# Moving the Q projection of the second half into the feature loop of the first, and rotating straight from PSUM

## What is computed

```python
h = _layernorm(x) * (1 + ca) + sa
q = h @ Wq.T + bq;  k = h @ Wk.T + bk;  v = h @ Wv.T + bv      # per head of 128
q = q*cos + _rotate_half(q)*sin;  k = k*cos + _rotate_half(k)*sin
qp, kp = features(q), features(k)     # x/|x|, @ R.T, then [sin, cos]/sqrt(F)
kv = einsum('bhsf,bhsd->bsfd', kp, v);  out = einsum('bhsf,bsfd->bhsd', qp, kv)
x = x + ga * (out @ Wo.T + bo)        # then layer norm 2 and the experts
```

## Time and profile before

| | us |
|---|---|
| median of the runs shown (2 runs: 3911.14 and 4193.43) | 4052.29 |
| the profiled execution, device time | 3917.5 |
| its span, slowest core (core 3) | 3915.9 |
| spans of the 8 cores | 3854.5 to 3915.9 |

### The profile page before, as it was taken

The page is one execution under the profiler, slowest core; times in us unless marked ns, Lnnn a source line. Parts: engine busy times, 40 slices in busy tenths (PEclk is TensorE's granted clock), DMA queues, the critical chain, the costliest instruction groups (busy, mean ns, idle before and its releaser), DMA issues.

```text
span 3915.9 us, 32272 instructions; the slowest of 8 cores (3854.5 to 3915.9 us)
## 1 busy us (share of the span) xinstructions
PE 2514.2 (64%) x10824; PEld 1084.3 (28%) x10824; DVE 1355.2 (35%) x2504; ACT 379.7 (10%) x422; POOL 169.7 (4%) x294
## 2 busy tenths in 40 slices
PE   3349721212982323493299678985899679976886
PEld 1124311101431111141144233432344234432332
DVE  0456255555623444536522122221222022211203
ACT  0111212121111101102100000000000000000000
POOL 0000000000000110000000000000000000000000
PEclk8559855555996566695599889998899789988998
DMA  9513100003325434710053675348543864457547
GB/s 161 104 54 65 25 26 15 27 15 56 56 52 92 85 74 81 174 22 0 16 108 70 131 240 128 75 84 239 172 92 65 184 217 99 92 111 226 156 74 270
DMA packets 84940, 395.10 MB, mean 101 GB/s; under 512 B 7184, under 2 KB 7440, under 8 KB 75312
## 3 DMA queue, kind: packets, MB, share of 16 engines
q0 software_dynamic: 41536, 208.26, 30.7%
q1 hardware_dynamic: 33696, 146.98, 10.9%
q10 hardware_dynamic: 9552, 37.80, 2.8%
HBM read 538.26 MB, written 46.20 MB: 149 GB/s over the span
## 4 chain that ended last, share of the span: by engine, by line
PE 51%; DMA 24%; DVE 13%; issue 8%; ACT 3%; DVEq 0%; POOL 0%; ACTq 0%; POOLq 0%; SPq 0%
PE pb L1034 23%; PE pb L612 9%; PE pb L1110 8%; DMA AW<-wmod 7%; DMA AW<-w2i 5%; DMA AW<-w2scr 5%; PE pb L902 3%; DVE AMS L780 2%; DMA w2scr<-AW 2%; PE pb L429 2%; DMA AW<-w1i 2%; PE pb L578 1%; DMA AW<-w3i 1%; PE pb L548 1%; DVE AMS L1122 1%
## 5 line engine op out<-in xcount | busy, mean ns | idle before, releaser
L1034 PE MATMUL pb<-AHT,AW 128*128 128x512 bf16 x4608 | 1007.8, 381 | 62.0 <-DMA AW<-w1i 39.6
L1110 PE MATMUL pb<-AW,AOT 128*128 128x512 bf16 x2304 | 593.5, 424 | 289.8 <-DMA AW<-w2i 154.3
L1034 PEld LDWEIGHTS pb<-AHT,AW 128*128 128x128 bf16 x4608 | 450.5, 98 | 619.1 <-issue 88.4
L1110 PEld LDWEIGHTS pb<-AW,AOT 128*128 128x128 bf16 x2304 | 241.9, 107 | 641.4 <-issue 432.6
L612 PE MATMUL pb<-AW,AHT 128*128 128x512 bf16 x1536 | 351.4, 382 | 0.0
L1122 DVE TENSOR_TENSOR AMS<-pb,AMS 128x2048 f32<-128x2048 f32 x40 | 91.6, 2291 | 727.8 <-PE pb L1110 724.4
L578 PE MATMUL pb<-identf,AX 128*128 128x128 f32 x256 | 98.6, 445 | 295.9 <-ACT AX L539 244.0
L429 PE MATMUL pb<-AW,scol 128*1 128x512 bf16 x384 | 135.0, 529 | 139.0 <-DMA AW<-wmod 122.9
L1058 ACT ACTIVATE AMS<-AMS 128x1024 f32<-128x1024 f32 x64 | 67.7, 1057 | 1470.2 <-DVE AMS L1055 1470.2
L1060 DVE TENSOR_TENSOR AMS<-pb,AMS 128x1024 f32<-128x1024 f32 x64 | 78.4, 1224 | 373.7 <-PE pb L1034 373.7
L612 PEld LDWEIGHTS pb<-AW,AHT 128*128 128x128 bf16 x1536 | 143.3, 98 | 182.5 <-issue 25.6
(11 more groups left out here) (148 smaller groups left out, 1666.8 us busy)
## 6 DMA issues: line engine op xcount, KB each, us to landing
AW<-w2scr SPq DMA_DIRECT2D x54, 2048.0 KB, 9.4
AW<-wmod POOLq DMA_DIRECT2D x24, 2048.0 KB, 19.4
w2scr<-AW ACTq DMA_DIRECT2D x18, 2048.0 KB
AW<-w1i POOLq DMA_DIRECT2D x32, 1024.0 KB, 8.1
AW<-w3i POOLq DMA_DIRECT2D x32, 1024.0 KB, 8.7
AW<-w2i POOLq DMA_DIRECT2D x16, 2048.0 KB, 24.2
AX<-xin SPq DMA_DIRECT2D x16, 1024.0 KB, 5.0
AW<-wqt POOLq DMA_DIRECT2D x4, 2048.0 KB, 18.2
```

The costliest lines, as they stand in the source:

```text
L1034: ins = tt.matmul(pu[:, th * 512:(th + 1) * 512], slot(sl)[:, ic * 128:(ic + 1) * 128], ahtb[:, ic * 1024 + th * 512: ic * 1024 + (th + 1) ...
L1110: ins = tt.matmul(pw[:, ob * 512:(ob + 1) * 512], hebuf[:, hc * 1024 + tau * 128: hc * 1024 + tau * 128 + 128], slot(ws)[:, ob * 512:(ob + ...
```

## The change

- `emit_qkv_block` is split into `emit_qkv_wdma` (the two loads) and `emit_qkv_chunk` (one tile's matmuls and what follows them). The bias load now takes lanes 4 to 7 as well.
- For q and k, the ACT copy to `srb` is gone in both halves; four of the six rotation operations on DVE read the float32 result in PSUM instead.
- Half 1's two q blocks move into half 0's feature loop: their weight and bias loads are emitted before the loop, and chunks (ob 0, tile t-1) and (ob 1, tile t-1) after `emit_ln1_tile(1, t)` in iterations 1 to 7; the last two come after `emit_mid_B(0, 7)`. Both chunks of an iteration use the same PSUM bank, `pqkv{(t-1)%2}`.
- The k and v blocks of half 1 stay behind the loop. The loads for ob 2 and 3 are emitted after the last q chunks, that for ob 4 after ob 2's chunks, that for ob 5 after ob 3's.

```diff
-        def emit_qkv_block(sh, ob):
+        def emit_qkv_wdma(sh, ob):
             wname, wbi = wsrc[ob]
             wkey = f"awblk{ob % 2}"
             sch.dma("gpsimd", lambda g, wname=wname, wbi=wbi, ob=ob: g.dma_start(
                 blkbuf(ob % 2)[:].rearrange("p (c n) -> p c n", c=NIC),
                 dram[wname][wbi]), lanes=(4, 5, 6, 7),
                 writes=W(ar_aw, wkey, (ob % 2) * 16384, (ob % 2 + 1) * 16384))
...
             sch.dma("gpsimd", lambda g, bsrc=bsrc, ob=ob, brow=brow: g.dma_start(
                 brow, dram[bsrc][0:1, (ob % 2) * 512:(ob % 2) * 512 + 512]),
-                writes=[brkey])
-            for t in range(8):
+                lanes=(4, 5, 6, 7), writes=[brkey])
+
+        def emit_qkv_chunk(sh, ob, t):
...
+            if True:
                 tg = sh * 8 + t
                 pcol = (t % 2) * 512
                 pv = pb0[:, pcol:pcol + 512]
...
-                    srb_ = srb if t % 2 == 0 else amsb[0:128, 14592:15104]
-                    srbk = "srb" + ("A" if t % 2 == 0 else "B")
-                    srb_lo = 19968 if t % 2 == 0 else 29184
-                    sch.op("scalar", lambda s, pv=pv, srb_=srb_: s.copy(srb_[:], pv),
-                           reads=[pk], writes=W(ar_ms, srbk, srb_lo, srb_lo + 1024))
+                    srbk = pk
...
-                    srb3 = srb_[:].rearrange("p (h d) -> p h d", h=4)
+                    srb3 = pv.rearrange("p (h d) -> p h d", h=4)
...
+        emit_qkv_wdma(1, 0)
+        emit_qkv_wdma(1, 1)
         for t in range(8):
             if t:
                 emit_mid_B(0, t - 1)
...
             emit_ln1_tile(1, t, True, None, lnxsA,
                           lambda: W(ar_x1, "lnxs", 57344, 65536),
                           cacol, sacol, ["col1", "col0"], vr=True)
+            if t:
+                emit_qkv_chunk(1, 0, t - 1)
+                emit_qkv_chunk(1, 1, t - 1)
         emit_mid_B(0, 7)
-        for ob in range(6):
-            emit_qkv_block(1, ob)
+        emit_qkv_chunk(1, 0, 7)
+        emit_qkv_chunk(1, 1, 7)
+        emit_qkv_wdma(1, 2)
+        emit_qkv_wdma(1, 3)
+        for t in range(8):
+            emit_qkv_chunk(1, 2, t)
+        emit_qkv_wdma(1, 4)
+        for t in range(8):
+            emit_qkv_chunk(1, 3, t)
+        emit_qkv_wdma(1, 5)
+        for t in range(8):
+            emit_qkv_chunk(1, 4, t)
+        for t in range(8):
+            emit_qkv_chunk(1, 5, t)
```

More of the change, by code:

```diff
@@ L595, in emit_qkv_block @@
                 writes=W(ar_aw, wkey, (ob % 2) * 16384, (ob % 2 + 1) * 16384))
-            isq, isv = ob < 2, ob >= 4
             bsrc = ["bq", "bq", "bk", "bk", "bv", "bv"][ob]
@@ L601, in emit_qkv_block @@
                 brow, dram[bsrc][0:1, (ob % 2) * 512:(ob % 2) * 512 + 512]),
-                writes=[brkey])
-            for t in range(8):
+                lanes=(4, 5, 6, 7), writes=[brkey])
+        def emit_qkv_chunk(sh, ob, t):
+            wkey = f"awblk{ob % 2}"
+            brow = brows[0:1, (ob % 2) * 512:(ob % 2) * 512 + 512]
+            brkey = f"brow{ob % 2}"
+            isq, isv = ob < 2, ob >= 4
+            if True:
                 tg = sh * 8 + t
@@ L657, in emit_qkv_block @@
                         writes=[dkey])
+        def emit_qkv_block(sh, ob):
+            emit_qkv_wdma(sh, ob)
+            for t in range(8):
+                emit_qkv_chunk(sh, ob, t)
         def emit_mid_A(sh, t):
```

## The result

The median of the kernel after is 3953.46 us (12 runs), that of the kernel before 3916.45 us (11 runs). The ratio is 1.0093, with a 95% interval of 1.0068 to 1.0118: about 36 us slower.

The account below looks back on a forecast made before the run. Latency was taken to bound the feature loop, no engine being full, and matmuls the projections; 3917.5 us plus 101.5 (loop), minus 38.4 (tail), minus 4 (bias lane) gave 3977 us, 1.5% more; 8-in-10 range 3945 to 4010.

Parts of the forecast that it names:

- the lower end, 3945: Whole kernel: low end of the 8-in-10 range, 3945 us, for chunks partly hidden in PE's idle time; hiding rival 5%.
- The place, and that nothing hides: Feature loop, behind emit_ln1_tile(1, t): chunks, rotation and products run serially, so PE's 10.0 us gap isn't free for q chunks.
- Price of a pair: Half 0's feature loop: 14.08 us for an iteration's two q chunks, 7 pairs; with bank waits +101.5 us.
- The second chunk at the full clock: Second q chunk of a loop iteration: 3.88 us, the clock still up after 2.5 us of idling; other end 5.58.
- the clock stays down: Rival, loop: half clock in both chunks, +5.06 us a pair, 4014 us (+2.5%); second chunk only, 3989; chance 17%.
- DVE reading PSUM: Rotation's four multiplies: float32 from PSUM costs the same as bf16 from SBUF, no change; upper end 7 us in all.
- The tail: Behind the loop, up to ob 2: fewer chunks left, but PE waits some 11 us for weights; -38.4 us, up to -28.
- The bias row's lane: Loads beside tile 1's x load: bias and second wqt load issued about 6 us earlier; 4 us off, ends 0 and 8.
- the sum itself: Whole kernel: +101.5 - 38.4 - 4 = +59.1 us on 3917.5, giving 3977 us, 1.5% more; forecast's chance 63%.
- a change of about 2%: Whole kernel: what a measurement can tell from none (to 3996 or 3839 us); chance of staying within it 0.80.
- lower ends (3945, 3965): Whole kernel: 3945 us starts the 8-in-10 range, for partial hiding; 3965 starts the forecast's own range, to 3996.

Follow-up runs that it names:

- e7: Kernel after, TensorE's semaphore waited for first, an iteration's two q chunks in two banks of the other PSUM tensor; ratio to kernel before 1.0034, loop 580 us.
- e9: Kernel after with two banks for the q chunks and their rotations emitted behind the products of the next emit_mid_B; ratio to kernel before 0.9896, loop 531 us.
- e6: Kernel after, TensorE's semaphore first, v blocks instead of q blocks in the loop, separate PSUM banks; no ratio, profiled run 3855.14 us, loop 495.4 us.
- e4: Kernel after with its wait order written out, TensorE's semaphore first and VectorE's last; ratio to kernel before 1.0095, loop 600.4 us.
- e2: Kernel before with the wait order written out, TensorE's semaphore first and VectorE's last; ratio to kernel before 0.9927, loop 496.0 us.
- e10: Kernel after with each engine's own semaphore waited for first and, of the others, VectorE's and TensorE's last; ratio to kernel before 1.0048.
- e5: Kernel before with each engine's own semaphore waited for first and, of the others, VectorE's and TensorE's last; ratio to kernel before 0.9884.
- e1: Kernel before with the wait order written out, VectorE's semaphore first and TensorE's last; ratio to kernel before 1.002.
- e3: Kernel after with the wait order written out, VectorE's semaphore first and TensorE's last; ratio to kernel before 1.0241.

## Why the prediction was right or wrong

It said 3977 us, 59 more than before. The time lies 36 us above, inside the range; the sign and the mechanism hold, the size doesn't, by 23 us. That it fell inside the range is luck: the lower end, 3945, stood for chunks that hide in part, and none did.

- **The place, and that nothing hides: right.** The timeline of after shows the chunks, the rotation and the products in a row. e7, e9 and e6 name the cause as the prediction did: the chunks cost 12.0 us a pair without the shared bank, 5.0 with the rotation behind the products, and 0 with nothing on DVE.
- **Price of a pair: right in sum.** +101.5 forecast, +104.4 measured at one wait order (e4 less e2), some 107 at another (e10 less e5). On core 3 the seven first chunks took 5.0 to 6.2 us (5.58 taken, ends 5.09 and 6.07), the gap for the bank 2.40 (2.5), the rotation as computed.
- **The second chunk at the full clock: wrong in part.** On core 3 two of seven second chunks took 5.3 us instead of 3.9, and so on 5 of the 7 other cores. In e4 it was two of seven on seven cores, in e10 three of seven on all eight, always behind the same gap of 2.40 us. The prediction took from the earlier trace rows that the clock holds for 2.7 us of idling, more than the 2.5 of the gap. Busy time by us of core 4 after the first chunk of another iteration, columns as in the earlier trace rows:

```profile
720.00:721.00 1.00, 1.00 (x6) 0.29 (x3) 0.00 (x0) 0.00 (x0) 0.00 (x0) 1.00 0.00 0
721.00:722.00 1.00, 0.23 (x1) 0.00 (x0) 0.67 (x2) 0.00 (x0) 0.00 (x0) 1.00 0.00 0
722.00:723.00 1.00, 0.00 (x0) 0.00 (x0) 0.79 (x3) 0.00 (x0) 0.00 (x0) 1.00 0.00 0
723.00:724.00 1.00, 0.38 (x1) 0.14 (x2) 0.90 (x3) 0.00 (x0) 0.00 (x0) 0.51 0.00 0
```

  PE stopped at 721.23, and at 723.0 the granted clock was down to half (1.2 GHz), after 1.8 us. One observation of 2.7 us was no bound. The miss costs 2 x 1.4 = 2.8 us, about what the loop measured more than the sum, and the third cold chunk of e10 fits its 107. It is a part of the rival "the clock stays down", at 2 of 7.
- **DVE reading PSUM: right, at no cost.** Groups by line, core 4, 520 to 1050 us:

```profile
L641 DVE TENSOR_TENSOR AMS<-pb,cosbuf 128x256 f32<-128x256 f32 x14 | 5.9, 425 | 66.7 <-PE pb L620 66.7
L644 DVE TENSOR_TENSOR AMS<-pb,sinbuf 128x256 f32<-128x256 f32 x14 | 5.8, 415 | 0.0
```

  425 and 415 ns out of PSUM, and 425 and 417 in the kernel before out of SBUF. By the estimate from the table in the Trainium skill, "VectorE: DVE Perf Modes", section "The TRN2 errata — SBUF-src ops pay a fixed extra latency per instruction", each would have been 0.065 us longer; neither size of operation shows it here.
- **The tail: right.** Ob 2 was to start 23.7 us after the loop, behind some 11 us of idling. It started 19.4 to 23.9 us after it, behind 7.2 to 11.7 us of idling (by core), and the slowest core is at the upper end. PE on core 4:

```profile
1057.17 5.27 PE L617 MATMUL pb<-AW,AHT 128*128 128x512 bf16 x15 [0.22 <-issue]
...
1065.15 3.61 PE L617 MATMUL pb<-AW,AHT 128*128 128x512 bf16 x16 [2.40 <-DVE AMS L653]
```

  and POOL:

```profile
1063.38 0.56 POOL L592 DMA_DIRECT2D AW<-wkt  x1 [81.09 <-PE pb L620]
...
1069.69 0.56 POOL L592 DMA_DIRECT2D AW<-wkt  x1 [5.23 <-PE pb L620]
```

  The loads are 6.3 us apart (6.4 forecast), and PE's second chunk ends at 1069.1; ob 2 starts at 1080.82, after 11.74 us that a load ends, by the profile the bias row right behind the weights. Loop and tail together, the third stage: +63.1 forecast, +65.5 at e2's and e4's order, +66.3 at e5's and e10's, +68.3 at e1's and e3's.
- **The bias row's lane: right in size.** -4 forecast; -2.7 with the lane alone, -4.7 in the whole change at one order (264.4 against 269.1), -5.6 at the other.
- **The step that failed is the sum itself, +101.5 - 38.4 - 4 = +59.1: it puts all the rest of the kernel at nothing, without a reason.** Its terms are sound: at a fixed wait order the change costs +64 to +66 us. What it left out is that the changed kernel is a new build with another order of waits: -29 us (e2, the kernel before with after's order written out, at 0.9927), over stages that no term spoke of (layer norm 1 -8.0, loop of half 0 -11, loop of half 1 -10.8, norm 2 with its surroundings -5.5, by e2 less before in one execution each, which adds up to 35). 59 - 29 = 30, plus 3 for the cold chunks, against 36 measured. The profile of before alone could have shown half of it: in its records of semaphores the met wait stands behind the late one 692 times on TensorE. It couldn't have shown what order the next build would take. The prediction had no rival for such a gain from outside the change, and its lower ends (3945, 3965) weren't made for it.
- **That only a change of about 2% can be told from none: wrong.** The interval of after is 0.25% to either side; +0.93% is plainly slower.

## What to carry over

Before work is moved into an engine's idle time, follow it through to the engine that the idle one is waiting for: moving q put 5.4 us of DVE work a tile in front of the operation that PE stood waiting on and lost 64 to 66 us, moving v into the same gap, with ACT as its only other engine and banks of its own, won 40. In a scheduler that turns dependencies into waits, fix their order, own semaphore and long-met ones first and the one expected last at the end: it was worth 1.2% here for a line or two, it is in no engine's busy time, and left to addresses it makes two builds of one source differ by more than many a change is worth. Compare two kernels only when the order of such waits is the same in both.

## What the hardware showed that I had not expected

- A wait that is already met costs TensorE 0.106 us when it stands behind one that was late (0.221 against 0.115 us from the end of L583 to the next weight load), and nothing that can be seen when it stands in front of it. On VectorE it costs 0.068 us (0.242 in e2 against 0.174 in e5, from TensorE's update to the small multiply L800).
- The granted clock fell to half after 1.8 us of idling in some gaps of 2.4 us and stayed up through others of the same length: 2 of 7 on six of the eight cores, none on the two others; 3 of 7 on all eight in e10. A chunk right behind it costs 1.4 us more. What decides between them stays open.
